# A fused transformer block on one core: first norm and first maxima taken apart, the shift row in the low half, biases added by products, and new instruction orders

## The reference

```python
mod = silu(c) @ wmod                      # six rows of 128: sa, ca, ga, sb, cb, gb
ga, gb = (sign(g) * max(|g|, 0.25) for g in (ga, gb))
h = layernorm(x) * (1 + ca) + sa
q, k, v = (h @ Wq + bq) / sqrt(128), h @ Wk + bk, h @ Wv + bv
weights = softmax(causal(q @ k.T))        # 2048 x 2048
x = x + ga * ((weights @ v) @ Wo + bo)
h = layernorm(x) * (1 + cb) + sb
mask = top 4 of 16 of softmax(h @ w_router + b_router)
y = sum over chosen blocks of relu(h @ w1_block + b1_block) @ w2_block
x = x + gb * (y + b2)
```

## Time and profile before

| | before |
|---|---|
| runs, us | 119.1, 118.75, 118.54 |
| median, us | 118.75 |
| span of the profiled execution, us | 117.1 |
| instructions in it | 1992 |
| busy us: PE, DVE, ACT, POOL | 110.9, 86.6, 75.4, 88.7 |
| HBM read, written, MB | 2.24, 1.05 |

### The profile page before, as it was taken

The page is one execution under the profiler, slowest core; times in us unless marked ns, Lnnn a source line. Parts: engine busy times, 40 slices in busy tenths (PEclk is TensorE's granted clock), DMA queues, the critical chain, the costliest instruction groups (busy, mean ns, idle before and its releaser), DMA issues.

```text
span 117.1 us, 1992 instructions
## 1 busy us (share of the span) xinstructions
PE 110.9 (95%) x583; PEld 87.7 (75%) x583; DVE 86.6 (74%) x312; ACT 75.4 (64%) x162; POOL 88.7 (76%) x122
## 2 busy tenths in 40 slices
PE   5998799999999999999999999999999999999980
PEld 1477675978888888878867987788889788865770
DVE  5669799998989989999888576825693945874521
ACT  2324968875984099559679959998075577536430
POOL 2566888999797989999896998999966798822000
PEclk9999999999999999999999999999999999999997
DMA  2796000000000000000000000000000000023033
GB/s 57 197 318 194 0 3 3 0 6 0 0 3 0 0 6 0 0 0 3 0 0 0 0 6 0 0 0 0 0 0 6 3 0 3 0 79 100 0 95 90
DMA packets 6290, 3.42 MB, mean 29 GB/s; under 512 B 1157, under 2 KB 5894, under 8 KB 6279
## 3 DMA queue, kind: packets, MB, share of 16 engines
q1 hardware_dynamic: 5846, 3.09, 9.2%
q10 hardware_dynamic: 432, 0.20, 0.6%
HBM read 2.24 MB, written 1.05 MB: 28 GB/s over the span
## 4 chain that ended last, share of the span: by engine, by line
PE 71%; POOL 13%; DVE 6%; ACT 4%; issue 4%; DVEq 0%
PE bank L848 17%; PE bank L852 17%; PE bank L849 16%; POOL p_lo L468 8%; PE bank L894 5%; PE bank L1116 4%; POOL rstd L393 3%; PE bank L965 2%; PE bank L875 2%; ACT xn L540 2%; PE bank L1053 2%; POOL neg_mean L391 1%; PE bank L1026 1%; ACT p_full L571 1%; DVE xn L649 1%
## 5 line engine op out<-in xcount | busy, mean ns | idle before, releaser
L468 POOL TENSOR_TENSOR p_lo<-p_full,p_hi 128x512 fp32r<-128x512 f32 (+2 forms) x36 | 42.4, 1202 | 3.9 <-ACT p_full L571 3.9
L564 ACT ACTIVATE p_hi<-bank 128x512 fp32r<-128x512 f32 (+2 forms) x36 | 20.7, 576 | 9.2 <-PE bank L852 4.6
L571 ACT ACTIVATE p_full<-bank 128x512 f32<-128x512 f32 (+2 forms) x36 | 20.6, 572 | 1.6 <-POOL p_lo L468 1.5
L474 POOL TENSOR_TENSOR hid_lo<-hid_full,hid_hi 128x512 fp32r<-128x512 f32 x12 | 15.8, 1321 | 3.9 <-ACT hid_hi L598 3.9
L675 DVE TENSOR_REDUCE cmax<-bank 128x1 f32<-128x512 f32 x24 | 16.1, 684 | 1.2 <-PE bank L894 1.0
L894 PE MATMUL bank<-zt_hi,g_hi 128*128 128x512 f32 (+3 forms) x40 | 15.6, 403 | 0.4 <-DVE g_hi L698 0.2
L848 PE MATMUL bank<-g_hi,zt_hi 128*128 128x512 f32 (+3 forms) x40 | 14.8, 370 | 0.0
L849 PE MATMUL bank<-g_hi,zt_lo 128*128 128x512 f32 (+3 forms) x40 | 14.6, 365 | 0.0
L852 PE MATMUL bank<-g_lo,zt_hi 128*128 128x512 f32 (+3 forms) x40 | 14.5, 363 | 0.0
L848 PE MATMUL bank<-p_hi,z_hi 128*128 128x512 f32 (+2 forms) x36 | 13.9, 385 | 0.0
L852 PE MATMUL bank<-p_lo,z_hi 128*128 128x512 f32 (+2 forms) x36 | 13.5, 376 | 0.1
(11 more groups left out here) (190 smaller groups left out, 255.9 us busy)
## 6 DMA issues: line engine op xcount, KB each, us to landing
x<-in_L_attn_y_all_dram SPq DMA_DIRECT2D x3, 256.0 KB, 3.9
out_dram<-res SPq DMA_DIRECT2D x3, 256.0 KB, 2.3
w<-in_L_ffn_w_dram SPq DMA_DIRECT2D x2, 256.0 KB, 5.0
x<-in_L_attn_y_all_dram SPq DMA_DIRECT2D x2, 128.0 KB, 2.9
...
wk<-in_L_attn_Wk_dram SPq DMA_DIRECT2D x1, 64.0 KB, 3.0
```

What stands on the lines that cost most here:

```text
L468: pool.tensor_tensor(p_lo[:, s, w:], p_full[:, n % 2, w:], p_hi[:, s, w:].bitcast(F32), ALU.subtract).then_inc(p_lo_pool, 1)
L474: pool.tensor_tensor(hid_lo[:, m, :], hid_full[:, n % 2, :], hid_hi[:, m, :].bitcast(F32), ALU.subtract).then_inc(hid_lo_pool, 1)
L564: nc.scalar.activation(p_hi[:, s, w:], src, ACT.Exp).then_inc(p_hi_s, 1)
L571: nc.scalar.activation(p_full[:, n % 2, w:], src, ACT.Exp).then_inc(p_full_s, 1)
```

## The change

Each part, in the order of the program:

- **Loads.** The columns bq, bk, bv (128 partitions of one element) and the row bo become rows of a zeroed tile bias_pad (partition 0, 128 elements each). SP waits for its memset (pads_made). wv is loaded before group 2 of x, which had come before wmod's second part.
- **Biases by products.** z10 (new on PE) writes the query and key biases into the banks as `bias_pad.T @ ident` and z1 adds to that; z4 and z5 have one such product more. ACT's with_bias (two operations a weight) becomes one copy; DVE's addition of bo goes.
- **silu** of c goes from POOL to DVE, with a reciprocal in place of the power −1. lift2 goes from DVE to ACT.
- **First norm in halves.** Statistics, power, application and the split into high and low are made for two tiles at a time (j, a, u on DVE; j on POOL and ACT), with two banks.
- **Norm 1** is applied by DVE (`v1`) instead of ACT. xn1 has four buffers instead of two, so the waits for a free one go, and the copy z_last goes with them.
- **First maxima** a0 to a3 go to four banks of their own, not through the two turned ones.
- **Shift row in the low half.** It is copied to row 0 of g_lo (0 before), not added to row 0 of g_hi. So only the third pass waits for it. For scores 0, 1, 2, 4, 5, 6 the first two passes are words of their own (`p`), placed ahead.
- **Weight products rehoused:** z4, z5 in norm_bank; z8, z9 in the bank of the weighed sum, behind the first group; so other steps wait for them now.
- **Fillers:** 7 of 512 columns instead of 10, 3 of 256 instead of 12. All four order lists are new.

```diff
-WAKE = 10
+WAKE = 7
-SCALAR_NORMS = (1, 2, 3, 4, 5, 6, 7)
+SCALAR_NORMS = (2, 3, 4, 5, 6, 7)
+SCORED_AHEAD = (0, 1, 2, 4, 5, 6)
+FIRST_MAXES = ("a0", "a1", "a2", "a3")
 TENSOR_PLAN = """
-i0 i1 i2 z0 i3 i4 i5 i6 i7 z1 n0 i8 i9 z2 i10 i11 z6 z3 z8 q0 z9 n1 a0 z4 a1 a2 q1 a3 z5 a4 z7 a5 b0 a6 n2 a7
+i0 i2 i1 z0 z10 z1 n0 z2 z3 q0 z6 z4 p0 a0 a1 a2 a3 p2 n1 z7 b0 q1 p1 s0 s1 s2 a4 z5 a5 s3 a6 a7 w0 n2 a8 a9 w1
...
-        xn1 = sb("xn1", [P, 2, GT, D])
+        xn1 = sb("xn1", [P, NG, GT, D])
...
+        def first_max_bank(k):
+            return (score_bank[2], score_bank[1], turn_bank[0], turn_bank[1])[k]
-        value_cols, back_cols, gate_cols = (score_bank[0][:, k * P:(k + 1) * P] for k in (1, 2, 3))
-        up_bank, down_bank = ctx_bank, score_bank[2]
+        value_cols = norm_bank[:, 0:P]
+        back_cols, gate_cols = (norm_bank[:, k * P:(k + 1) * P] for k in (0, 1))
+        up_bank, down_bank, router_cols = ctx_bank, ctx_bank, ctx_bank[:, 0:NBLK]
+        def first_bank(i):
+            return (norm_bank, turn_bank[1])[i]
...
             load(wk[:], wk_in, wk_in_s)
-            load_column(BQ, bq_in, bias_qk_in_s)
-            load_column(BK, bk_in, bias_qk_in_s)
+            sp.wait_ge(pads_made, 1)
+            load_bias(BQ, bq_in, bias_qk_in_s)
+            load_bias(BK, bk_in, bias_qk_in_s)
...
+            def first_half_power(i):
+                t = slice(2 * i, 2 * i + 2)
+                pool.wait_ge(stats if i else first_stats, 1)
+                step(pool.tensor_scalar(rstd[:, 0, t], mv[:, 0, t, 1], EPS, None, ALU.add))
+                pool.tensor_tensor(rstd[:, 0, t], rstd[:, 0, t], pow_half[:, 0:2], ALU.pow).then_inc(power_s if i else first_power, 1)
...
-                ahead(pool.tensor_copy(z_last[:, g, :], norm_rows(g)[:, GT - 1, :]))
...
+            def first_stat(i):
+                dve.wait_ge(x_in_s[0] if i else x_first_s, 16)
+                for t in (2 * i, 2 * i + 1):
+                    last = nc.vector.bn_stats(st[:, 0, t, :], x[:, t, :])
+                step(last)
+                for t in (2 * i, 2 * i + 1):
+                    last = nc.vector.bn_aggr(mv[:, 0, t, :], st[:, 0, t, :])
+                last.then_inc(stats if i else first_stats, 1)
...
                 if one_turn(g):
                     for r in range(GT):
-                        top = tile(g_hi, g * GT + r)[0:1, :]
-                        last = nc.vector.tensor_tensor(top, src[Q * r:Q * r + 1, 0:P], top.bitcast(F32), ALU.add)
+                        last = nc.vector.tensor_copy(tile(g_lo, g * GT + r)[0:1, :], src[Q * r:Q * r + 1, 0:P])
...
+                if i == 0:
+                    dve.wait_ge(exp_c_s, 1)
+                    step(nc.vector.tensor_scalar(silu[:, 1:2], silu[:, 0:1], 1.0, None, ALU.add))
+                    step(nc.vector.reciprocal(silu[:, 2:3], silu[:, 1:2]))
+                    nc.vector.tensor_tensor(silu[:, 3:4], cols[:, C:C + 1], silu[:, 2:3], ALU.mult).then_inc(silu_s, 1)
...
-            def score(t):
+            def first_passes(t):
                 g, j = tile_of[t]
                 w = from_col[t]
                 dst = score_bank[t % SCORE_BANKS]
...
+                high = g_hi[:, g * GW + w:(g + 1) * GW]
+                mm(dst[:, w:], tile(zt_hi, j), high, start=True, stop=False)
+                mm(dst[:, w:], tile(zt_lo, j), high, start=False, stop=False)
...
+                elif i == 10:
+                    pe.wait_ge(ident_made, 1)
+                    pe.wait_ge(bias_qk_in_s, 32)
+                    mm(score_bank[1][:, 0:P], bias_pad[:, BQ, :], ident[:], start=True, stop=False)
+                    mm(score_bank[2][:, 0:P], bias_pad[:, BK, :], ident[:], start=True, stop=False)
...
                     pe.wait_ge(wv_in_s, 16)
-                    pe.wait_ge(fold_lo_s, 1)
-                    mm(value_cols, wv[:], lift1[:], start=True, stop=True).then_inc(wv_mm, 1)
+                    pe.wait_ge(bias_vo_in_s, 32)
+                    pe.wait_ge(nt_lo_s, 1)
+                    mm(value_cols, wv[:], lift1[:], start=True, stop=False)
+                    mm(value_cols, bias_pad[:, BV, :], ident[:], start=False, stop=True).then_inc(wv_mm, 1)
```

More of the change, by code:

```diff
@@ L64 @@
-k6 k7 k8 k9 k10 k11
+z7 z0 z4 z8 j0 j1 z1 p1 p2 z6 u0 l0 l1 l2 p3 u1 l4 l5 l6 l7 l8 z11 l9 l10 z10 u2 l12 l13 l14 l15 l16 p4 l17 l18
+l19 l20 l21 p5 l22 z9 l24 l25 l26 l27 l28 p6 l29 l30 k0 l31 l32 l33 l34 l35 k1 u3 l36 l37 l38 k2 k3 k4 k5 p7 k6
+k7 k8 k9 k10 k11
 """
@@ L118, in adaln_attention_sparse_ffn @@
     for word in TENSOR_PLAN.split():
-        if word[0] in "aboh":
+        if word[0] in "aboh" and word not in FIRST_MAXES:
             turn_of[word] = turns
@@ L344, in load_x, with load_bias @@
                 load(tokens(x, g), x_tiles[g], x_in_s[g])
+            def load_bias(n, src, done):
+                load(bias_pad[0:1, n, :], row(src), done)
             for i in range(2):
@@ L486, in _ @@
             nc.scalar.activation(warm[:, 1:2], warm[:, 0:1], ACT.Exp)
-            def with_bias(dst, src, n, done):
-                nc.scalar.activation(dst[:, 0:1], src[:, 0:1], ACT.Identity, bias=cols[:, n:n + 1])
-                nc.scalar.copy(dst[:, 1:], src[:, 1:P]).then_inc(done, 1)
             def prepare(i):
@@ L505, in prepare @@
                 elif i == 4:
-                    act.wait_ge(bias_vo_in_s, 32)
                     act.wait_ge(wv_mm, 1)
-                    with_bias(wv_t, value_cols, BV, wv_t_s)
+                    nc.scalar.copy(wv_t[:], value_cols).then_inc(wv_t_s, 1)
                 elif i == 5:
@@ L542, in apply, with first_high @@
                 last.then_inc(xn_by_act, 1)
+            def first_high(i):
+                half = slice(i * GW // 2, (i + 1) * GW // 2)
+                act.wait_ge(xt_mm if i else first_turned, 1)
+                nc.scalar.copy(zt_hi[:, half], first_bank(i)[:, 0:GW // 2]).then_inc(nt_hi_s if i else first_hi, 1)
             def norm_high(n):
@@ L653, in apply, with first_low @@
-                if n > 0:
-                    last.then_inc(xn_by_dve, 1)
+                for i in range(GT):
+                    t = n * GT + i
+                    last = nc.vector.tensor_scalar(norm_rows(n)[:, i, 1:], x[:, t, 1:], mv[:, 0, t, 0:1],
+                                                   rstd[:, 0, t:t + 1], ALU.subtract, ALU.mult)
+                last.then_inc(xn_by_dve, 1)
+            def first_low(i):
+                half = slice(i * GW // 2, (i + 1) * GW // 2)
+                dve.wait_ge(nt_hi_s if i else first_hi, 1)
+                last = nc.vector.tensor_tensor(zt_lo[:, half], first_bank(i)[:, 0:GW // 2], zt_hi[:, half].bitcast(F32),
+                                               ALU.subtract)
+                if i:
+                    last.then_inc(nt_lo_s, 1)
@@ L829, in _ @@
             nc.vector.memset(xn2[:, :, :, 0:1], 1.0)
+            nc.vector.memset(bias_pad[:], 0.0).then_inc(pads_made, 1)
             nc.vector.memset(keys[:], FURTHEST).then_inc(keys_made, 1)
@@ L950, in weigh @@
                     pe.wait_ge(p_hi_s, t + 1)
-                    mm(ctx_bank[:, w:], z_last[:, g, :], p_last[:], start=False, stop=True).then_inc(pv_done, 1)
+                    mm(ctx_bank[:, w:], norm_rows(g)[:, GT - 1, :], p_last[:], start=False, stop=True).then_inc(pv_done, 1)
                     return
```

218 lines of the change are left out of this document (116 added, 102 removed).

## The result

The changed kernel takes **120.87 us** (median, 120.65 to 121.48), the kernel before 118.78 beside it: ratio 1.018, interval 1.014 to 1.022. It is 1.8% slower, where 117.05 was forecast, and lies outside the range.

A forecast was written before the change was run, and what follows sets the result against it. PE, 95% busy, was taken to bound the kernel: a dense row of products behind a head chained over four engines. Span 117.1 − 2.3 + 0.6 = 115.4, with 1.65 to the median: 117.05 us; range 115.9 to 118.9.

The forecast's parts named there:

- The steps of the head: Start to score 4: first projection at 9.45 instead of 11.51, shift row 16.1 (19.67), first exponential 16.8 (20.97).
- Score 4 is whole: End of the head: score 4 complete at 25.9 us, against 27.4 before, 1.45 of time gained.
- The shift row's copy: Head, turned shift row: copying 512 elements from a bank taken at 0.68, the price of the addition it replaces.
- PE's lead in equal work is 2.3: At score 4: 1.45 us of time plus 0.9 of products already done puts PE 2.3 us ahead.
- less 0.6 for DVE: Behind score 4: DVE must take 1.9 from idle time up to 60 us; loss between 0 and 1.9, taken 0.6.
- the tail is the same: End of the kernel: y3, y4 and the last stores unchanged, no time added.
- rival 3: Behind the head: new orders open PE holes at scores whose bank isn't free, 0.3 to 0.5 each; 118.7 us; chance 0.13.
- doesn't hold PE: POOL, with u3 moved behind k1: l12 can start at 39.4 instead of 42.71, and POOL doesn't hold PE.
- By the row of the norm nothing is added.: Norm 1 on DVE beside POOL: no cost; by the skill's lock rule, total perhaps 0.3 worse.
- Rival 2: Head: with fewer fillers PE's clock rises late, doubling products; 120.5 us in full, chance 0.07; in part no change, 0.06.
- Rival 1: Up to 60 us: DVE binds and nearly all 1.9 is lost; gain 0.2 to 0.7, 118.3 us; chance 0.14.
- The mark that was to show it wrong: PE between 28 and 60 us: forecast wrong if its holes there sum to over 1.5.

The follow-up runs named there:

- e9: e1 with ten wake-up fillers in place of seven; 117.48 us (0.987).
- e10: The changed kernel with three more waits on GpSimd, which keep its next instruction behind each `chosen` comparison; 120.21 us (1.011).
- e13: e2 with GpSimd's waits for the first two `chosen` comparisons and ten fillers; 118.97 us (1.000).
- e12: The changed kernel with the old order between head and b3, u3 early, GpSimd's waits for the first two `chosen`, and ten fillers; 118.63 us (0.998).
- e14: e12 with the old lists again behind o3, so only b3 to o3 is new; 118.48 us (0.999).
- e2: The changed kernel with POOL's list alone changed: u2 behind u1, u3 ahead of l12 instead of behind k1; 120.10 us (1.013).
- e5: The changed kernel with five small moves on PE alone, putting products in front of words that waited; 121.47 us.
- e6: e2 with the old order in all four lists behind b3; 118.88 us (0.999).
- e8: The changed kernel with DVE's `chosen` made by comparing two tensors instead of a tensor with a scalar; 121.53 us.
- e11: The changed kernel with ten wake-up fillers in place of seven; 120.56 us.
- e4: e1 with u3 late, ahead of l36, and u2 ahead of l12; 118.06 us (0.997).
- e1: The changed kernel up to PE's a24, the four old order lists behind it, u2 and u3 early; 117.92 us (0.992).

## Why the prediction was wrong

**The steps of the head held.** None of its marks is off by more than 0.6 us. Score 4 is whole at 25.88, as forecast; the 27.4 of the kernel before was counted to the start of the next product, and by the listed end it is 27.52, so the time gained there is 1.6 to 1.7 and not 1.45. The shift row's copy did cost the 0.68 of the addition.

**"PE's lead in equal work is 2.3", less 0.6 for DVE: about right, for another kernel.** e9 has the changed head and, behind a24, the lists of before (and ten fillers). Its b3 stands 1.74 us earlier than before's and its last y 1.67. Forecast was 2.3 − 0.6 = 1.7. That the profiles give just this is in part luck: e9's profiled execution (117.24) was its quickest, and before's span, 117.1, is 0.2 above that of most of its executions. In medians it is 1.2.

**The step that failed is the one that isn't there.** The sum 117.1 − 2.3 + 0.6 has no term for the new orders behind the head. They fill most of the four lists, and got nothing; "the tail is the same" was said of y3 and y4 and let stand for all of it. They appear only as rival 3, at 0.13, with four holes of 0.3 to 0.5. Measured, those behind a24 take 3.5 us in profile (last y 115.65 against e9's 112.14), and so:

- up to b3, 0.7 us (49.06 − 1.20 against 47.17 from the head's mark), with holes at s12 and n4 (that at s24 is just behind b3). Rival 3's mechanism, an engine behind PE, is right there, but PE waits for DVE's shift row and for norm 4, not for a score's bank;
- b3 to o3, 2.8 us (33.47 + 1.20 against 31.88). Of it 1.5 are the three lock-outs (e10, 31.99), 0.1 what u3's place adds to that (e13, 31.86), and 1.2 a rest, of the size that e12 shows (1.23), whose cause stays open but for single holes (here s24's, 0.46; in e14 the two named above);
- behind o3, nothing measurable.

The hole at n4 (0.62 at 51.29) has a lock-out behind it as well, which no run of its own tested. The new list of DVE has the addition of the w1 bias at 43.48, beside GpSimd's splits, and one of these then takes 2.16 in place of 1.29:

```profile
43.48 1.60 DVE L852 TENSOR_TENSOR w_full<-w_full,b_row 1x512 f32<-1x512 f32 x1
```

```profile
44.09 2.16 POOL L490 TENSOR_TENSOR p_lo<-p_full,p_hi 128x512 fp32r<-128x512 f32 x1
```

In the chain above these are the five splits from 40.35, 7.17 us where the earlier trace rows have 6.29, and norm 4's power, its application and n4 follow them. All eight profiles with the new list up to b3 (the changed kernel, e2, e5, e6, e8, e10, e11, e13) have a split of 2.14 to 2.17 there, and the seven that leave n4 in its new place have a hole of 0.59 to 0.63 ahead of it; of the kernels with the old order there none has either.

**That GpSimd, with u3 behind k1, "doesn't hold PE" was wrong.** u3's late place costs 0.9 us with the old orders (e4) and 0.8 with the new ones (e2). In the new ones two causes are tangled: in the changed kernel the third comparison was locked out for 1.59 us, in e2 it took 0.43, and in e11, with u3 late, 0.43 as well, with 32.93 us from b3 to o3 against e2's 32.92. So of what e2 won there, 0.55, most or all may be that GpSimd was out of the way.

**"By the row of the norm nothing is added."** I weighed the lock at one place, norm 1, where the row spoke against it, and priced it at 0 to 0.3. There it held: beside norm 1 (11.10 to 12.18) GpSimd's first two operations took 0.24 and 0.37, against 0.24 and 0.23 beside none at 47.60, 0.13 us in all. The place where it decides was not on any list of mine: an unchanged instruction, 40 us and more behind the head, whose neighbour on GpSimd now starts (at the second) 0.08 us ahead of it in place of 0.09 behind. A hint stood in the earlier trace rows, neg_mean at 0.95 in place of 0.25.

**Rival 2, the clock late, is real and small.** It came in six of the nine profiled executions with seven fillers, though not in the changed kernel's own, and costs 0.9 to 1.2 us at the projection; in the changed kernel's median it is some 0.3 (e11), which is not clear of noise. In e1 it ends at 9.91, before the projection, so the 3.5 us of doubled work, which had the maxima in them, never came together. Rival 1 is out as the main cause: DVE's busy time from 28 to 60 fell by 0.7, and e9, with the same head, keeps 1.7 in profile.

**The mark that was to show it wrong did.** Holes of PE between 28 and 60 were to stay under 1.5 us in sum; they are 1.6. That the larger part would come behind 60, where "both have room", I had excluded by the averages of the earlier trace rows.
